# Attention: the product of probabilities and values issued in two halves of 256 queries, in TensorE's hand-written order

## The reference

```python
keys = x @ jnp.triu(Wk).T ; queries = x @ jnp.tril(Wq).T ; values = x @ Wv.T   # x: layer-normed
dot = jnp.einsum('bqhs,bkhs->bhqk', queries, keys) * scale      # 16 heads, 2048 x 2048
att = jax.nn.softmax(dot, axis=-1)
out = jnp.einsum('bhqk,bkhs->bqhs', att, values).reshape(b, t, e)
return out @ Wu.T + bu
```

## Time and profile before

| | us |
|---|---|
| median of 3 runs | 1668.05 |
| lowest, highest | 1664.76, 1669.87 |
| span of the profiled execution (first to last instruction) | 1666.9 |
| attention stage in it | about 0 to 715 |
| TensorE, VectorE, ScalarE, GpSimd busy | 1519.7, 1383.8, 920.8, 296.9 |
| mean granted TensorE clock | 0.954 |

### The profile page before, as it was taken

The page is one execution under the profiler, slowest core; times in us unless marked ns, Lnnn a source line. Parts: engine busy times, 40 slices in busy tenths (PEclk is TensorE's granted clock), DMA queues, the critical chain, the costliest instruction groups (busy, mean ns, idle before and its releaser), DMA issues. The chain is left out here.

```text
span 1666.9 us, 24179 instructions
## 1 busy us (share of the span) xinstructions
PE 1519.7 (91%) x8562; PEld 759.0 (46%) x8562; DVE 1383.8 (83%) x2459; ACT 920.8 (55%) x1751; POOL 296.9 (18%) x364
## 2 busy tenths in 40 slices
PE   6899999999999999979997888976999869989699
PEld 2111111111111111268883333322888758869587
DVE  6999999999999999476664999999766657787686
ACT  3088888888888888832224765754322232222232
POOL 3200000000000000000013788784000200020000
PEclk7599999999999999989998999999999979999799
DMA  3340000100000001000001222220000003200123
GB/s 95 102 159 24 24 30 27 31 27 25 24 24 24 24 24 49 9 1 1 1 1 41 73 64 72 67 67 26 1 1 1 1 1 103 81 23 1 52 78 103
DMA packets 41315, 65.92 MB, mean 40 GB/s; under 512 B 11444, under 2 KB 18661, under 8 KB 40490
## 3 DMA queue, kind: packets, MB, share of 16 engines
q1 hardware_dynamic: 41194, 64.37, 12.6%
HBM read 56.68 MB, written 6.75 MB: 38 GB/s over the span
## 5 line engine op out<-in xcount | busy, mean ns | idle before, releaser
L844 DVE TENSOR_REDUCE row_max<-ps 128x1 f32<-128x1024 f32 x512 | 601.2, 1220 | 33.4 <-PE ps L641 17.4
L758 ACT ACTIVATE probs<-ps 128x512 f32<-128x512 f32 x944 | 487.8, 603 | 119.7 <-PE ps L656 119.4
L641 PE MATMUL ps<-k_stack,q_stack 48*128 48x512 bf16 x1024 | 325.0, 402 | 20.4 <-DVE row_max L844 10.6
L656 PE MATMUL ps<-q_stack,k_stack 51*128 51x512 bf16 x944 | 322.1, 387 | 2.2 <-ACT probs L758 0.2
L585 PE MATMUL ps<-probs,v_head 128*16 128x512 f32 x2048 | 269.8, 599 | 1.3 <-issue 1.1
L641 PEld LDWEIGHTS ps<-k_stack,q_stack 48*128 48x128 bf16 x1024 | 58.5, 95 | 368.0 <-DVE row_max L844 342.0
L1373 PE MATMUL ps<-s_hc,ident 128*128 128x512 f32 x256 | 139.0, 628 | 47.9 <-DVE s_hc L1646 42.9
L1026 ACT ACTIVATE x_gate<-ps 128x512 f32<-128x512 f32 x128 | 76.5, 599 | 184.5 <-PE ps L122 184.4
L1298 POOL TENSOR_TENSOR s_dbx<-s_dx,s_b_rows 128x512 f32<-128x512 f32 x128 | 159.4, 1270 | 35.2 <-DVE s_h L1637 34.7
L1637 DVE TENSOR_TENSOR_SCAN s_h<-ps,s_state,s_dbx 128x512 f32<-128x512 f32 x128 | 157.3, 1274 | 4.6 <-POOL s_dbx L1298 2.8
L1063 DVE TENSOR_TENSOR x_hidden<-x_gate,ps 128x512 f32<-128x512 f32 x128 | 87.2, 686 | 53.4 <-PE ps L122 42.5
(11 more groups left out here) (345 smaller groups left out, 1935.1 us busy)
## 6 DMA issues: line engine op xcount, KB each, us to landing
s_b_rows<-s_b_dram SPq DMA_DIRECT2D x64, 256.0 KB, 3.1
y_spread<-y_probs_dram SPq DMA_DIRECT2D x128, 128.0 KB, 2.9
q_stack<-q_parts_dram SPq DMA_DIRECT2D x30, 96.0 KB
k_stack<-k_parts_dram SPq DMA_DIRECT2D x30, 96.0 KB
w_w<-w_dram SPq DMA_DIRECT2D x1, 2048.0 KB, 8.0
q_stack<-q_parts_dram SPq DMA_DIRECT2D x30, 64.0 KB
k_stack<-k_parts_dram SPq DMA_DIRECT2D x30, 64.0 KB
o_dram<-o_sb SPq DMA_DIRECT2D x60, 32.0 KB
```

Of the source, the lines that this page charges most:

```text
L641: last = nc.tensor.matmul(core.ps[:, 2 * b + r, :], qst[buf][0:KROWS, u * P:(u + 1) * P], kst[buf][0:KROWS, key:key + CH], start=True, sto ...
L656: nc.tensor.matmul(core.ps[:, S_BANK + n % S_RING, :], kst[buf][HALF:ROWS, kt * P:(kt + 1) * P], qst[buf][HALF:ROWS, c * CH:(c + 1) * CH], ...
L758: nc.scalar.activation(probs[:, us % RING, c * CH:(c + 1) * CH], core.ps[:, S_BANK + n % S_RING, :], ACT.Exp).then_inc(exp_done, 1)
L844: nc.vector.tensor_reduce(mx[:, u, b:b + 1], core.ps[:, 2 * b:2 * b + 2, :], mybir.AxisListType.XY, ALU.max).then_inc(max_done, 1)
```

## The change

With `of=2` a unit's value product is issued in two parts: part 0 covers queries 0 to 255 of each chunk and comes behind find and score 1, part 1 covers queries 256 to 511 and comes behind find and score 3. Each part has four calls (eight matmuls, eight weight loads) with 256 columns. Units with kt = 0, whose first matmul opens the accumulation in the bank, are issued whole, now behind find and score 1. The waits stand ahead of part 0, `pv_done` is counted after part 1. The calls in the tail keep the defaults (whole). Slots with values and finds number 234, of them 15 with kt = 0.

```diff
-            def weigh_values(m):
+            def weigh_values(m, part=0, of=1):
                 buf, kt = m // NT % NBUF, m % NT
-                if kt == 0:
-                    pe.wait_ge(v_staged, m // NT + 1)
-                    if m:
-                        pe.wait_ge(evacuated, m // NT)
-                pe.wait_ge(exp_done, 4 * m + 4)
+                if part == 0:
+                    if kt == 0:
+                        pe.wait_ge(v_staged, m // NT + 1)
+                        if m:
+                            pe.wait_ge(evacuated, m // NT)
+                    pe.wait_ge(exp_done, 4 * m + 4)
+                width = CH // of
+                cut = slice(part * width, (part + 1) * width)
                 for c in range(NC_):
-                    last = nc.tensor.matmul(core.ps[32 * c:32 * c + VROWS, O_BANK, :], v_head[buf][:, kt, :],
-                                            probs[:, m % RING, c * CH:(c + 1) * CH],
-                                            start=kt == 0, stop=kt == NT - 1)
-                last.then_inc(pv_done, 1)
+                    last = nc.tensor.matmul(core.ps[32 * c:32 * c + VROWS, O_BANK, cut], v_head[buf][:, kt, :],
+                                            probs[:, m % RING, c * CH:(c + 1) * CH][:, cut],
+                                            start=kt == 0, stop=kt == NT - 1 and part == of - 1)
+                if part == of - 1:
+                    last.then_inc(pv_done, 1)
@@ in slot, inside the loop over c
                     if scores:
                         score(c)
-                if values:
-                    weigh_values(j * BODY + gs - LAG_V)
+                    if values and (gs - LAG_V) % NT == 0:
+                        if c == 1:
+                            weigh_values(j * BODY + gs - LAG_V)
+                    elif values and c % 2:
+                        weigh_values(j * BODY + gs - LAG_V, c // 2, 2)
```

## The result

| | before | changed |
|---|---|---|
| median of runs, us | 1668.72 (4 runs) | 1638.16 (4 runs, 1637.41 to 1639.47) |
| ratio, 95% interval | | 0.9827 [0.9811, 0.9842] |
| span of the profiled execution | 1666.9 | 1635.9 (its own time 1637.65) |
| end of the attention stage | 716.28 | 685.68 |

The change makes the kernel 30.6 us faster. The whole difference lies in the stage that was changed: it ends 30.60 us earlier, and what comes after it takes 950.2 us where it took 950.6.

The account below looks back on a forecast made before the run. It took score 0, exponential 0, score 3 and all values as the bound; 548.5 + 7.0 + 4.9 = 560.4 us against 572.9 gained 12.5, with +0.45 and -0.25 making 12.7: 1655.4 us, range 1650 to 1668.

Parts of the forecast that it names:

- The ring: Attention loop: score 0, exponential 0, score 3, all eight value matmuls, next score 0; 2.44 us, the whole slot.
- The next bound: Attention loop after the change: VectorE's own two reductions, 1.177 us each, 2.354 per slot.
- that very cycle: Attention loop: reduction end to find to next reduction of the same banks, 1.91 us against VectorE's 2.354.
- Head end: End of each head on VectorE: two small operations cost 0.50 us, 14 times, untouched by the change.
- Stall: Slot with kt = 0: VectorE waits 0.35 us for find 2 behind the whole batch, once for each of 14 heads.
- Half batch: Half of a unit's value matmuls, from first matmul to next find: 0.55 to 0.59 us, taken as 0.57.
- TensorE's half slot: TensorE's own sum in the loop without waits: 0.55 for two pairs plus 0.57 for values, 1.12 us.
- Edges: Outside the steady loop: first value batch in slot 22 loses 0.25 us (stall 1.05 to about 1.3), tail gains 0.45.
- Larger stalls: Rival, chance 0.12: VectorE waits 0.8 us at each head's kt = 0 slot; time 1661.7 us.
- drain: Rival, chance 0.12: each change of shape on TensorE waits for the whole previous record; slot 2.45, time 1666 to 1669.
- cost by instruction: Rival, chance 0.10: a 256-column value batch costs more than 0.69 us; about 1802 us at the ceiling, 1701 if mild.
- no stall beyond today's: Low end of the forecast's own range, 1650 us, with the half value batch at its floor; present wait 0.22 per head.

Follow-up runs that it names:

- exponential 0 against exponential 1: Kernel before, with ScalarE taking only 256 of 512 queries in the exponential of chunk 0 (1636.11 us) or of chunk 1 (1666.16 us) in looped units.
- the second kernel with added matmuls: Changed kernel with one added 128 x 128 by 128 x 512 matmul of real values behind each pair of finds in slots 8 to 19: 1644.57 us.

## Why the prediction was right in sign and wrong in size

*The bound: right.* The ring was read correctly from one slot, and exponential 0 against exponential 1 shows it. The change works by cutting it: the wait of the scores for exponentials fell from 70.1 to 6.5 us in 420.

*The next bound: wrong, and this is the failed step.* "20 reductions take 23.58 us ... 1.177 each, 2.354 per pair" took a run without visible idle time for VectorE's own rate. That run lies in a stretch at the 1.2 GHz level, where a pair of finds takes 1.03 and closes a cycle of 2.33 around each pair of banks. I had worked out that very cycle for the loop (1.22 + 0.05 + 0.64 = 1.91) at the 2.4 GHz level and did not redo it for the stretch from which I took the rate. The right number stood in the earlier trace rows as well: 299.51 to 300.65, a step of 1.14 inside a slot, shorter than the "floor" of 1.177. Measured, the pair is 2.263. On 233 slots that is 233 x 0.091 = 21.2 us.

*The terms again, with what they measured.* Loop from slot 23: 233 x 2.263 = 527.3, 14 head ends, 14 stalls; the trace has 90.88 to 633.06, 542.2 us, where the forecast was 560.4. Head end 0.58 instead of 0.50 (the last reduction's 1.25 is to be set against 1.13, not 1.21). Stall 0.46 instead of 0.35, in the slot that was named and for the reason named: counted from find 0, batch, find 2 and reduction come at 0.96, 1.94 and 2.58, forecast 0.95, 1.93 and 2.57, and halving those slots removes the stall. The 0.11 more is the same wrong rate again: a faster VectorE is ready for the pair 0.10 earlier. 527.3 + 8.1 + 6.4 = 541.8 closes the sum.

*Half batch: right.* 0.56 and, where TensorE waits behind it, 0.59; taken 0.57. TensorE's half slot 1.10 against 1.12. On changes of tiling mode, the Trainium skill, TensorEngine Tiling (Array Packing), Key Properties, says that they drain TensorE. The runs bear out a small price at most: the fixed part of a batch is 0.12, and the way in costs 0.09 more than between scores. It is not a wait for the end of the records, since the batch of 300.57 is recorded until 301.20 and the next find starts at 301.13. What of the 0.12 belongs to the change of mode was not separated.

*Edges: right within 0.3.* First batch: the stall is 1.57 instead of 1.05, so 0.5 lost instead of 0.25. From the last reduction to the end of the stage 52.98 before, 52.62 after: 0.36 gained, 0.45 forecast, and what is late next is the load of the last maxima, as said (scores of the last head at 640.00, a wait of 1.13 for `max_dram`).

*The rivals.* Larger stalls, drain and cost by instruction all went the slow way; none of them happened beyond about a tenth of a microsecond (the stall, 0.11 a head). No case on the fast side had been allowed for, since 1.177 was taken as a floor without bounds. The range ended at 1650, "no stall beyond today's", all with the same wrong rate; and that label is loose: 1655.4 less all 14 x 0.35 is 1650.5, while today's 0.22 would have given 1653.6.

## What to carry to other kernels

An engine's own step is at most the shortest one between like instructions anywhere in the trace (1.14 here), not the average of a run that shows no idle time (1.177); where records overlap, waits of up to 0.1 us vanish in them, so read single starts, and ask of any "undisturbed" stretch at which clock the other engine ran. With three buffers for four scores, the long block was in a ring in both places where it was put; cutting it, or shortening the one exponential in its ring, took the ring out of the bound. Another buffer might too; no run here shows it. To find whether an engine's work is in the ring, shorten one instruction in it and one beside it.

## What the runs showed of the hardware that I had not expected

- TensorE stayed at the 1.2 GHz level from about 25 to 90 us while busy 84 to 86% of the time with finds and value projections, and up to 100% in three kernels with added 128 x 128 by 512 bf16 matmuls, with zeros or with real values alike. In all thirteen traces it rose to the 2.4 GHz level only 1.4 to 3.4 us after the start of the first float32 value batch (an estimate from the granted clock in stretches of 2 us). That start ranges from 85.54 to 94.83 us, and the rise goes with it: 0.98 over 90 to 92 us in the changed kernel (batch at 86.85), 0.50 up to 96 and 0.94 over 96 to 98 us in the second kernel with added matmuls (batch at 94.83). So the time from the start alone doesn't decide. The first scores, 5 to 7 us ahead of the batch, move along with it in these kernels; whether it was they or the batch is open.
- A reduction of 1024 columns is recorded as 1.21 to 1.23 us, but the next starts 1.13 after it: 0.08 overlap. A shortening by 64 columns took 0.07 off the record (1.15 to 1.16) and off the step (13 reductions in 13.95 instead of 14.80 us).
